# Fused two-layer attention kernel: the last two tiles of the q, k, v products reordered, self-attention's turns moved inside them, and its row sums and the starts of two later phases rewritten

## The reference, cut to what matters

```python
x = rms_norm(hidden_states, ln_in_w)
mixed = jnp.where(vm, x @ v_qkv, x @ l_qkv)        # two experts, chosen per token
q, k, v = jnp.split(mixed, 3, axis=-1)             # 16 heads of 32
q, k = apply_rotary(q, k, position_ids, l)
ctx = sdpa(q, k, v, causal=True)                   # self-attention, softmax over 112 keys
hidden_states = residual + jnp.where(vm, ctx @ v_dense, ctx @ l_dense)
ci = rms_norm(hidden_states, ln_post_cross_w)
cctx = sdpa(ci @ cq_w, *split(encoder_outputs @ ckv_w), causal=False)   # 16 heads of 16
hidden_states = hidden_states + cctx @ cdense_w
# then a gated MLP, again with one of two experts per token
```

## Time and profile before

| what | value |
|---|---|
| median of 3 executions | 2189.94 us (2188.38 to 2192.73) |
| the profiled execution | 2186.0 us |
| its span in the profile | 2184.1 us |
| TensorE busy | 2096.5 us, 96% |
| VectorE, ScalarE, GpSimd busy | 1276.0, 1049.1, 876.5 us |
| phase B's last two tiles | about 533 to 582 us |
| phase C | about 584 to 816 us |
| phase D, phase E | about 816 to 981 us, 981 to 1490 us |

### The profile page before, as it was taken

One profiled execution on the slowest core, in us unless ns is written; L12 is line 12 of the kernel. 1 busy time (PEld: TensorE's weight loads), 2 busy tenths in 40 slices (PEclk: granted clock), 3 DMA queues, 4 the chain that ended last, 5 costly groups with the idle time before them and its releaser, 6 DMA issues.

```text
span 2184.1 us, 40739 instructions
## 1 busy us (share of the span) xinstructions
PE 2096.5 (96%) x16042; PEld 1815.5 (83%) x16042; DVE 1276.0 (58%) x2070; ACT 1049.1 (48%) x1875; POOL 876.5 (40%) x741
## 2 busy tenths in 40 slices
PE   8999999999888989997999999989999999999998
PEld 7899988888677768886989989977888888888888
DVE  6655657665589994445667667663434434443333
ACT  5444444433277765443566556554433334343334
POOL 2210128677444334552121111104455554555547
PEclk9999999999899999998999999999999999999999
DMA  6443526565654446556887777745343443434434
GB/s 243 138 172 108 181 105 202 199 240 209 201 160 138 142 159 245 226 197 198 238 239 218 218 218 221 211 134 188 106 142 124 146 141 106 143 121 126 118 92 131
DMA packets 155614, 373.70 MB, mean 171 GB/s; under 512 B 40160, under 2 KB 60992, under 8 KB 145696
## 3 DMA queue, kind: packets, MB, share of 16 engines
q1 hardware_dynamic: 136416, 310.70, 45.0%
q0 software_dynamic: 18720, 60.29, 7.6%
q10 hardware_dynamic: 288, 0.11, 0.0%
HBM read 269.28 MB, written 100.93 MB: 170 GB/s over the span
## 4 chain that ended last, share of the span: by engine, by line
PE 80%; DVE 8%; DMA 5%; ACT 3%; SPq 2%; issue 2%; POOL 0%; POOLq 0%; ACTq 0%; DVEq 0%
PE ps L111 20%; PE ps L113 20%; PE ps L112 20%; PE ps L1853 4%; PE ps L1885 3%; PE ps L1872 3%; DMA f_arena<-qk_rows 2%; DVE f_arena L1311 2%; DVE c_max L1306 2%; PE ps L687 2%; ACT f_arena L1767 1%; DMA f_arena<-weights 1%; PE ps L1230 1%; PE ps L1900 1%; PE ps L2201 1%
## 5 line engine op out<-in xcount | busy, mean ns | idle before, releaser
L111 PE MATMUL ps<-r_arena 128*128 128x512 f32 (+6 forms) x2410 | 890.3, 369 | 13.9 <-DVE r_arena L179 8.6
L113 PE MATMUL ps<-r_arena 128*128 128x512 f32 (+6 forms) x2410 | 880.2, 365 | 0.0
L112 PE MATMUL ps<-r_arena 128*128 128x512 f32 (+6 forms) x2410 | 879.7, 365 | 0.0
L179 POOL TENSOR_TENSOR r_arena<-f_arena,r_arena 128x512 fp32r<-128x512 f32 (+1 forms) x434 | 576.6, 1353 | 530.4 <-ACT r_arena L201 408.1
L111 PEld LDWEIGHTS ps<-r_arena 128*128 128x128 f32 (+2 forms) x2410 | 453.6, 188 | 77.4 <-issue 6.7
L113 PEld LDWEIGHTS ps<-r_arena 128*128 128x128 f32 (+2 forms) x2410 | 453.0, 188 | 65.5
L112 PEld LDWEIGHTS ps<-r_arena 128*128 128x128 f32 (+2 forms) x2410 | 454.1, 188 | 60.0
L201 ACT CAST r_arena<-f_arena 128x512 fp32r<-128x512 f32 x400 | 236.5, 623 | 175.4 <-PE ps L113 129.6
L1979 DVE TENSOR_REDUCE e_negmax<-ps 112x2 f32<-112x750 f32 (+1 forms) x352 | 240.5, 721 | 94.7 <-PE ps L1853 93.4
L2289 DVE SCALAR_TENSOR_TENSOR f_arena<-f_arena,ps 128x512 f32<-128x512 f32 (+1 forms) x88 | 57.4, 653 | 235.1 <-ACT f_arena L2184 230.6
L1767 ACT ACTIVATE f_arena<-ps 125x896 f32<-125x896 f32 x192 | 166.3, 923 | 45.0 <-PE ps L1872 45.0
(11 more groups left out here) (213 smaller groups left out, 2566.2 us busy)
## 6 DMA issues: line engine op xcount, KB each, us to landing
f_arena<-weights SPq DMA_DIRECT2D x400, 256.0 KB, 2.9
r_arena<-k_rows SPq DMA_DIRECT2D x192, 188.0 KB, 3.6
k_rows<-r_arena SPq DMA_DIRECT2D x64, 376.0 KB
f_arena<-rows SPq DMA_DIRECT2D x14, 1160.0 KB, 5.2
f_arena<-qk_rows SPq DMA_DIRECT2D x32, 448.0 KB, 4.0
f_arena<-mem_n SPq DMA_DIRECT2D x8, 1536.0 KB, 6.7
f_arena<-mem_e SPq DMA_DIRECT2D x32, 376.0 KB, 4.7
f_arena<-mem_t SPq DMA_DIRECT2D x16, 750.0 KB, 5.5
```

The source lines that it names most:

```text
L111: first = pe.matmul(out, w_hi, x_hi, start=start, stop=False)
L112: pe.matmul(out, w_hi, x_lo, start=False, stop=False)
L113: return first, pe.matmul(out, w_lo, x_hi, start=False, stop=stop)
L179: return engine.tensor_tensor(out, source, high.bitcast(F32), ALU.subtract)
```

## The change

- **Phase B**: the order of (tile, chunk) pairs becomes a list, `b_order`: tiles 0 to 5 as before, then q and k of tile 6, q and k of tile 7, v of tile 6, v of tile 7. Chunk numbers and counts follow the list. Tile 7 gets its own value rows and other banks. `b_sin` shrinks to one buffer, and each block's `rope` waits for the one before. GpSimd scatters q and k rows of tiles 6 and 7 before the value rows of both. The four low parts that VectorE makes come after its last `rope`. The last product of the list is issued by phase C's code, between the turning of q and k of batch 0 and of batch 1. ScalarE copies tile 7's values out after batch 0's q and k.
- **Phase C**: SyncE loads q and k of batches 0 and 1 when the q and k rows have landed (it no longer waits on the last two tiles' values for batch 2 either). `shift` is done in two halves, and the masks wait for one half each. GpSimd folds all 16 heads, from 112 to 56 and then to 28 columns; VectorE sums 16 x 28 in one instruction. The turning in of q comes between the second and third quarter of the context, that of k after the fourth; ScalarE's copies follow.
- **Phase D**: tile 7's queries have a buffer of their own, so ScalarE's copy does not wait for the scatter of tile 6.
- **Phase E**: of the six DMAs that place batch 0's queries, ScalarE's queue issues three instead of two; for batches 1 and 2 ScalarE's queue issues the six query DMAs. In steps 30 and 31 units 4 and 5 of the scores come before `back`.

```diff
+        b_sin = fv(19312, (HEADS, HD))
+        b_vs_last, b_ids = fv(20304, (TB // 2, VROW)), fv(19824, (TB,))
+        b_order = [(n, c) for n in range(TILES - 2) for c in range(B_CHUNKS)]
+        b_order += [(n, c) for n in (TILES - 2, TILES - 1) for c in range(2 * KT)]
+        b_order += [(n, c) for n in (TILES - 2, TILES - 1) for c in range(2 * KT, B_CHUNKS)]
+        b_place = {key: m for m, key in enumerate(b_order)}
...
+        def b_bank(n, which, j):
+            if n + 1 == TILES:
+                return (0, 4, 4)[which] + (2 * j if which == 2 else j)
+            return 4 * ((n + which) % 2) + j
...
@@ b_pool
-                store(n)
+                store_roped(n)
+                if n + 2 < TILES:
+                    store_values(n)
+            store_values(TILES - 2)
+            store_values(TILES - 1)
@@ b_product (from b_pe)
+            for j in range(tb(n)):
+                x = slice(j * P, (j + 1) * P)
+                if c == 0 and final:
+                    pe.wait_ge(b_roped, 2 * blocks(n - 1) + j + 1)
...
+                if c == KT and final:
+                    pe.wait_ge(b_roped, 2 * blocks(n - 1) + tb(n - 1) + j + 1)
+                if c == 2 * KT and final:
+                    pe.wait_ge(b_roped, 2 * blocks(n) + tb(n) + 1)
+                elif c == 2 * KT and last_two:
+                    pe.wait_ge(b_roped, 2 * blocks(n + 1) + min(j + 1, tb(n + 1)))
...
@@ rope
-                    by_sin = b_sin[j % 2]
+                    by_sin = b_sin
+                    if n or which or j:
+                        dve.wait_ge(b_roped, 2 * blocks(n) + which * tb(n) + j)
@@ b_dve
                 rope(n, 1)
+                if n + 1 == TILES:
+                    dve.wait_ge(w_lo_made, b_chunk(n, RING))
+                    for c in range(RING, B_CHUNKS):
+                        ring_low(dve, b_chunk(n, c))
@@ c_sp
             sp.wait_ge(b_scattered, 16 * BLOCKS)
+            sp.wait_ge(b_v_scattered, 16 * blocks(TILES - 2))
             for b in range(2):
                 load_qk(b)
+            sp.wait_ge(c_tk, 1)
+            load_qk(2)
             sp.wait_ge(b_v_scattered, 16 * BLOCKS)
@@ c_pool, fold
-                half = c_prob[b % 2][:, HEADS // 2:HEADS, :]
-                pool.tensor_tensor(c_fold, half[:, :, 0:SEQ // 2], half[:, :, SEQ // 2:SEQ], ALU.add).then_inc(c_folded.sem, 1)
+                half, quarter = SEQ // 2, SEQ // 4
+                pool.tensor_tensor(c_fold, c_prob[b % 2][:, :, 0:half], c_prob[b % 2][:, :, half:SEQ], ALU.add).then_inc(c_folded.sem, 1)
+                pool.wait_ge(*c_folded.at(2 * b + 1))
+                pool.tensor_tensor(c_fold[:, :, 0:quarter], c_fold[:, :, 0:quarter], c_fold[:, :, quarter:half], ALU.add).then_inc(
+                    c_folded.sem, 1)
@@ c_act, step s
+                if s + 1 < BATCHES:
+                    keys(s + 1)
...
                 if s:
                     act.wait_ge(c_ctx, s)
                     act.copy(c_ctx_raw, ps[:, 6, 0:NT].rearrange("p (t s) -> p t s", t=KT)).then_inc(c_raw, 1)
+                if s + 2 < BATCHES:
+                    queries(s + 2)
                 if s < BATCHES:
-                    act.wait_ge(c_shifted, s + 1)
+                    act.wait_ge(c_shifted, 2 * (s + 1))
@@ c_pe
-            pe.wait_ge(b_v, BLOCKS)
-            turn_in(0)
-            turn_in(1)
+            turn_queries(0)
+            turn_keys(0)
+            b_product(pe, *b_order[-1])
+            turn_queries(1)
+            turn_keys(1)
+            pe.wait_ge(b_v, blocks(TILES - 1))
             for s in range(BATCHES + 2):
                 if s < BATCHES:
-                    masks(s)
+                    masks(s, 0)
                 if s >= 2:
                     turn_out(s - 2)
                 if s < BATCHES:
+                    masks(s, 1)
                     scores(s)
...
+                if 1 <= s <= BATCHES:
+                    context(s - 1, 0)
+                    context(s - 1, 1)
                 if s + 2 < BATCHES:
-                    turn_in(s + 2)
+                    turn_queries(s + 2)
                 if 1 <= s <= BATCHES:
-                    for j in range(QUADS):
-                        context(s - 1, j)
+                    context(s - 1, 2)
+                    context(s - 1, 3)
+                if s + 2 < BATCHES:
+                    turn_keys(s + 2)
@@ c_dve
+                for half in range(2):
+                    j = slice(2 * half, 2 * half + 2)
+                    dve.tensor_tensor(c_prob[b % 2].rearrange("p (m j) s -> p m j s", j=4)[:, :, j, :], now[:, :, j, :],
+                                      c_max[:].rearrange("p (m j) -> p m j", j=4)[:, :, j].unsqueeze(3).to_broadcast([SEQ, KT, 2, SEQ]),
+                                      ALU.subtract).then_inc(c_shifted, 1)
             def sums(b):
-                dve.wait_ge(c_exp, b + 1)
-                dve.tensor_reduce(c_sum[:, 0:HEADS // 2], c_prob[b % 2][:, 0:HEADS // 2, :], AX_X, ALU.add).then_inc(c_summed, 1)
-                dve.wait_ge(*c_folded.at(b + 1))
-                dve.tensor_reduce(c_sum[:, HEADS // 2:HEADS], c_fold, AX_X, ALU.add).then_inc(c_summed, 1)
-                dve.wait_ge(c_summed, 2 * (b + 1))
+                dve.wait_ge(*c_folded.at(2 * (b + 1)))
+                dve.tensor_reduce(c_sum[:], c_fold[:, :, 0:SEQ // 4], AX_X, ALU.add).then_inc(c_summed, 1)
+                dve.wait_ge(c_summed, b + 1)
@@ d_act
-                    if n >= 2:
+                    if 2 <= n < TILES:
                         act.wait_ge(*d_scattered.at(16 * blocks(n - 1)))
@@ e_act, steps 0 and 1
+                if s + 1 < ALONE:
+                    act.wait_ge(*e_cleared.at(1 if s == 0 else 3))
+                    act.wait_ge(*stored(s + 1))
+                    place_rows(act, s + 1)
@@ e_pe, step s
                 if new:
                     e_key_products(pe, s + 2)
+                elif now:
+                    scores(s, 4)
+                    scores(s, 5)
                 if old:
                     back(s - 2)
...
-                if now:
+                if new:
                     scores(s, 4)
                     scores(s, 5)
```

More of the change, by code:

```diff
@@ L1143, in c_sp @@
                 load_v(b)
-            for b in range(2, BATCHES):
+            for b in range(3, BATCHES):
                 sp.wait_ge(c_tk, b - 1)
@@ L1224, in turn_in @@
                 if b in (1, 2):
-                    pe.wait_ge(c_k, b)
-                for bank, at, turned, turn in ((5, 0, c_tq, 1), (7, DIM, c_tk, 2)):
-                    if b >= 3:
-                        pe.wait_ge(c_pt_made, QUADS * (b - 3) + turn + 1)
-                    for t in range(KT):
-                        last = pe.transpose(ps[:, bank, batch(t)], c_qk[b % 2][:, at + t * P:at + (t + 1) * P],
-                                            ident[0:SEQ, 0:SEQ])
-                    last.then_inc(turned, 1)
@@ L1234, in masks, with turn_keys @@
-            def masks(b):
+                    pe.wait_ge(c_q, b)
+                if b >= 3:
+                    pe.wait_ge(c_pt_made, QUADS * (b - 3) + 2)
+                for t in range(KT):
+                    last = pe.transpose(ps[:, 5, batch(t)], c_qk[b % 2][:, t * P:(t + 1) * P], ident[0:SEQ, 0:SEQ])
+                last.then_inc(c_tq, 1)
+            def turn_keys(b):
+                if b in (1, 2):
+                    pe.wait_ge(c_k, b)
+                if b >= 3:
+                    pe.wait_ge(c_pt_made, QUADS * (b - 3) + 3)
+                for t in range(KT):
+                    last = pe.transpose(ps[:, 7, batch(t)], c_qk[b % 2][:, DIM + t * P:DIM + (t + 1) * P], ident[0:SEQ, 0:SEQ])
+                last.then_inc(c_tk, 1)
@@ L1235, in masks @@
+            def masks(b, half):
                 if b:
-                    pe.wait_ge(c_shifted, b)
-                for j in range(4):
+                    pe.wait_ge(c_shifted, 2 * (b - 1) + half + 1)
+                for j in (2 * half, 2 * half + 1):
                     pe.matmul(ps[0:SEQ, j, 0:NT], ident_b[0:SEQ, 0:SEQ], causal[:].rearrange("p m s -> p (m s)"),
@@ L1647, in rows_of, with place_queries, place_rows @@
             return x[3 * t + part:MAX_ROW:PARTS]
-        def place_queries(engine, part, source):
-            for t in range(CT):
+        def place_queries(engine, part, source, tiles):
+            for t in tiles:
                 engine.dma_start(rows_of(e_queries[0], t, part)[:, t].bitcast(F32), source[:, t, queries].bitcast(F32)).then_inc(
                     e_placed[0].sem, 16)
+        ALONE = 3
+        def place_rows(engine, b):
+            into, done = e_queries[b % 3].rearrange("p t g s -> p t (g s)").bitcast(F32), e_placed[b % 2].sem
+            for t in range(CT):
+                for part, x in enumerate((0, 0, 1)):
+                    engine.dma_start(rows_of(into, t, part)[:, t], q_rows[b, t, x]).then_inc(done, 16)
         def e_sp(sp):
@@ L1686, in place_both @@
                 place_keys(b)
```

(10 more changed lines are left out.)

175 lines of the change are left out of this document (92 added, 83 removed).

## The result

| kernel | median of runs | span profiled |
|---|---|---|
| before | 2189.19 us (5 runs, 2185.62 to 2192.73) | 2184.1 us |
| after | 2175.98 us (5 runs, 2175.43 to 2176.73) | 2173.7 us |

The ratio is 0.994, with a 95% interval of 0.9929 to 0.9951: faster, by 13.2 us of medians and 10.4 us of profiled span. The forecast was 28.2 us and 2161.7 us. The sign held, less than half of the size came, and the median lies at the very end of the range.

A forecast was written before the change was run, and what follows sets the result against it. TensorE, busy 96%, was taken to bound the kernel; in C, VectorE's row sums and an equal 6.59 us loop. 9.2 + 17.1 - 1.4 + 3.3 = 28.2 off 2186.0 gave 2157.8, plus 3.9 for the median: 2161.7 us, range 2151 to 2176.

The forecast's parts named there:

- Part 1: C's start: scores of batch 0 end 8.5 us earlier, those of batch 2 another 0.7; gain 9.2.
- the new wait: Before v of tile 6: with one `rope` buffer, TensorE waits for a bank; 1.9 us lost.
- The bound of 4 of Part 1: C's start: the gain is only 4 us instead of 9.2 if the loads are late by 5.
- Part 2: 29 steps of C: 6.71 us becomes 6.12, TensorE binding, 0.10 of it load waits; gain 17.1, bounds 9 and 22.
- a step near 6.4: Rival, steps of C: a hand-over counted as just in time is not; gain 9 instead of 17.1, 2170 us; chance 0.22.
- Part 3: C's end: `context_low` stands behind row sums that wait for both folds; 1.4 us lost.
- Its bound of 4 with a falling clock: C's end: up to 4 us lost instead of 1.4 if the clock falls in the gap.
- Part 4: D to E: placements 0.65, ScalarE's DMAs 1.1 and steps 30 and 31 1.6 give 3.3 us; bounds 0 and 7.
- The placements: E's start: SyncE issues three of batch 0's placements instead of four; gain 0.65 us.
- ScalarE's transfers: E's start: 3.9 us of issues make ScalarE's split 1.1 late but remove TensorE's 2.16 wait; gain 1.1.
- The slower rival: Steps of C: q, k landings lengthen once TensorE asks sooner; a loss above 5.7 us, 2204 at 6.2; chance 0.04.
- Folds blocking the shift: Rival, steps of C: GpSimd's folds block VectorE's shift; its step is 6.8, part 2 gives -3, 2182 us; chance 0.04.

The follow-up runs named there:

- e1: The kernel after, with the ten weight loads spread over later steps of C instead of one block behind q, k of batch 3; median 2173.72 us.
- e6: The kernel before with only the new tile order and the early turns and loads; step of C, D and E as before; median 2188.89 us.
- e4: The kernel after, with SyncE issuing q, k of batch b + 1 ahead of v of batch b; median 2171.67 us.
- e3: The kernel after, with query rows of batches 1 and 2 issued by SyncE again, as before; median 2173.05 us.
- e7: The kernel after with weight loads spread, q, k ahead of v, tile 6's v in row-block order 2, 3, 0, 1, and batches 1 and 2's query rows on SyncE; 2160.39 us.

## Why the prediction was wrong

The forecast missed 17.8 us of span, of which the milestones place nearly all. Up to the last scores it had 9.2 + 17.1 = 26.3 and 10.9 came. The step that failed most is the jump from batch 2's scores to a steady step, the second point below.

- **Part 1, C's start.** Right: the new wait (1.9 forecast, 1.85 measured), the vanished wait for q and k, the last scatter at 572.8 (573.34). Too small by 1.9: v of tile 6, which the sum puts at 578.4, came at 580.7. The clock fell behind the wait (0.63 in [568:572]), which cost 1.6 of it in this profile; in five others with the same waits it did not fall, so this part is chance of the execution that was profiled. So batches 0 and 2 came 6.6 earlier, not 8.5 and 9.2: **2.6 short**.
- **The boundary between Parts 1 and 2.** The sum jumped from batch 2's scores to a steady step and took the loads in between as the earlier trace rows showed them. The bound of 4 of Part 1 was for loads "late by 5", but of batch 0, not 4. The ten weight loads that SyncE issues after q, k of batch 3 cost nothing before, because C began late and TensorE asked for batch 4 only when they had landed. An earlier C moves the asking, not the weights. Batch 2 to 3 took 14.02 us instead of 6.12: **7.9 short**, 5.57 of it waiting and the rest work at half clock. e1 and e6 show it: with the weights later the wait is gone, and with the new start alone it is there.
- **Part 2, the step.** The bound was right: TensorE, 6.02 forecast, 6.07 measured; folds 2.2 and 1.14 forecast, 2.09 and 1.15 measured; VectorE freed. The waits were mis-sized: 0.10 a step forecast, 5.22/28 = 0.19 measured, with a median landing of 4.5 instead of 4.0. Mean 6.29 instead of 6.12, over 28 steps **4.8 short**: 2.4 by the waits, 1.4 by the bound, and 1.0 in the steps around the waits. The rival with "a step near 6.4" has the size, but not for its reason: e4 without load waits runs at 6.07.
- **Part 3, C's end.** 1.1 lost, 1.4 forecast. Its bound of 4 with a falling clock is real too: six of seven kernels with this step paid 1.4 to 2.8 more, and the profiled execution of the kernel after did not.
- **Part 4, E.** From the first turn to F's first turn 500.58 became 499.70: 0.9 instead of 3.3, **2.4 short**. The placements gave 0.36 instead of 0.65. ScalarE's transfers were given +1.1 and cost about 1.4 (e3): the six issues took 4.68 us, not 3.9, and TensorE's 2.16 came back as 2.73 for VectorE. In step 30 a wait of 1.03 for `q_rows` ate much of the rest.
- The slower rival (landings stretch once TensorE asks sooner) had the mechanism that ruled: it was priced as a rule for every step, against a median, and never asked at which step the queue would be full. Folds blocking the shift: refuted. The 64 halves of the shift took 1.080 to 1.093 us each, 29 of them with a fold or another GpSimd instruction beside them for over 0.8 us.

Sum of the shortfalls: 2.6 + 7.9 + 4.8 + 2.4 = 17.7. C's end came 0.3 better than forecast, and phase F, which the change leaves alone, took 0.4 longer.

## What to carry to other kernels

When work is pulled forward, follow each queue that feeds it past the point where the gain is booked: a burst of transfers that was free because nobody was waiting becomes the next wait, here 5.57 us of waiting and 2.3 more behind it, at half clock. Book a gain at the end of the phase, not at its first milestone. Two equal limits need both edits, and several small waits are worth testing together: e7's four edits gave 15.6 us by medians, clear of the noise, where three of the four single gains were not. And before a fall of the clock in one profile is booked to a wait, look for the same wait in the profiles of the other kernels.

## What was not expected of the hardware

- TensorE got one load 10.15 us after its issue behind ten others on the same queue, with a median landing of 4.5, while the DMA share stood at 1.04 to 1.06; in e4 the load behind it has a recorded landing of 13.3.
- The same short waits were followed by a fall of the granted clock in some profiles and not in others. Behind 0.6 + 1.2 us before tile 6's v it fell to 0.50 for about 3 us in two of seven; behind 2.0 + 1.1 (0.6 in e7) at C's end it fell in six of seven; behind the wait of 2.69 before tile 1 of D in ten of the fourteen that have it.
- Six issues took ScalarE 4.68 us once and 3.88 the next time. SyncE's six of keys took 4.38 beside ScalarE's, but also 3.68 to 5.21 in the kernel before with nothing beside them, so no cost of issuing from two engines at once is shown.
- Filling idle TensorE with products that nobody reads saved about 2 us at C's end, where the chain behind the gap is TensorE's own, and 1.2 in E's first turns; at C's start nothing shows, and by medians no filled place but C's end went with a lower time.
